# The first two groups of edges in another order, statistics by halves, and idle transposes, in a graph layer with experts

## What is computed

```python
xn = layernorm(x)                                   # no weights
m_in = concat([xn[src], edge_attr], axis=1)         # 2500 x 640
m = relu(m_in @ W1.T + b1) @ W2.T + b2
agg = segment_sum(m, dst, num_segments=10000)
gi = agg @ W_ih.T + b_ih                            # three gates of 512
gh = xn @ W_hh.T + b_hh
r = sigmoid(i_r + h_r); z = sigmoid(i_z + h_z); n = tanh(i_n + r * h_n)
h_new = (1 - z) * n + z * xn
x = x + xn + gamma * (h_new - run_mean) * rsqrt(run_var + 1e-5) + beta
x = x + top2_of_8_experts(layernorm(x)) + 0.5 * shared_expert
```

## Time and profile before

| | us |
|---|---|
| median of 3 runs | 1423.47 |
| lowest, highest | 1421.75, 1424.54 |
| the profiled execution's own time | 1422.28 |
| its span, first to last instruction | 1420.5 |
| PE busy | 1356.3 (95%) |
| DVE, ACT, POOL busy | 1030.6, 738.2, 827.6 |
| first matmul of `layer1(0)` | 23.34 |
| end of the last `sums` | 336.04 |
| first matmul of the nodes | 370.75 |

### The profile page before, as it was taken

The page is one execution under the profiler, slowest core; times in us unless marked ns, Lnnn a source line. Parts: engine busy times, 40 slices in busy tenths (PEclk is TensorE's granted clock), DMA queues, the critical chain, the costliest instruction groups (busy, mean ns, idle before and its releaser), DMA issues.

```text
span 1420.5 us, 22825 instructions
## 1 busy us (share of the span) xinstructions
PE 1356.3 (95%) x6398; PEld 1088.8 (77%) x6398; DVE 1030.6 (73%) x2194; ACT 738.2 (52%) x1665; POOL 827.6 (58%) x1119
## 2 busy tenths in 40 slices
PE   4889999999889999999999999999999999999996
PEld 3668888887668777877787778777777777777774
DVE  3586444233478888888888888888888888888885
ACT  3431323212466566656665666566666666666552
POOL 3210242103477777777777777777777777777771
PEclk9999999999989999999999999999999999999997
DMA  8222534246423333333333333333333333333330
GB/s 311 69 68 88 185 135 144 90 152 244 163 97 126 119 132 112 127 116 133 113 129 112 133 118 125 111 133 118 125 111 133 119 124 112 131 122 122 114 109 30
DMA packets 62863, 179.57 MB, mean 126 GB/s; under 512 B 9328, under 2 KB 9968, under 8 KB 62704
## 3 DMA queue, kind: packets, MB, share of 16 engines
q1 hardware_dynamic: 46912, 99.20, 20.4%
q0 software_dynamic: 15920, 79.97, 16.4%
HBM read 141.86 MB, written 37.29 MB: 126 GB/s over the span
## 4 chain that ended last, share of the span: by engine, by line
PE 89%; DVE 4%; issue 2%; DMA 1%; ACT 1%; POOL 1%; POOLq 0%; SPq 0%; DVEq 0%; ACTq 0%
PE bank L1547 45%; PE bank L1584 9%; PE bank L1214 8%; PE bank L1594 8%; PE bank L526 6%; PE bank L1166 5%; PE bank L1184 4%; PE bank L1197 3%; PE bank L1596 1%; POOL whh_lo_raw L766 1%; PE bank L1148 1%; DVE st_e L890 1%; DMA late_out<-gates_in,carry_at 1%; DMA whh_lo_raw<-in_whh_t 0%; DVE found L957 0%
## 5 line engine op out<-in xcount | busy, mean ns | idle before, releaser
L1547 PE MATMUL bank<-whh_hi,x_hi 128*128 128x512 f32 x948 | 382.5, 403 | 10.8 <-DVE x L1493 10.5
L1547 PE MATMUL bank<-whh_hi,x_lo 128*128 128x512 f32 x948 | 375.3, 396 | 0.0
L1547 PE MATMUL bank<-whh_lo,x_hi 128*128 128x512 f32 x948 | 375.2, 396 | 0.0
L1547 PEld LDWEIGHTS bank<-whh_hi,x_hi 128*128 128x128 f32 x948 | 178.5, 188 | 51.6 <-DVE x L1493 10.9
L1547 PEld LDWEIGHTS bank<-whh_hi,x_lo 128*128 128x128 f32 x948 | 178.4, 188 | 43.5
L1547 PEld LDWEIGHTS bank<-whh_lo,x_hi 128*128 128x128 f32 x948 | 178.7, 189 | 39.1
L1295 POOL TENSOR_TENSOR rstd<-var_eps,minus_half 128x1 f32<-128x1 f32 x158 | 90.6, 574 | 149.5 <-DVE var_eps L479 149.5
L1346 POOL TENSOR_TENSOR h_n<-h,n_gate 128x512 f32<-128x512 f32 x79 | 103.9, 1315 | 58.6 <-ACT n_gate L1402 58.6
L504 ACT ACTIVATE h<-xt,shift,rstd 128x512 f32<-128x512 f32 x79 | 64.5, 816 | 134.1 <-POOL one_rstd L1301 134.1
L1286 POOL DMA_INDIRECT gates<-gates_in,slot_at x79 | 85.3, 1079 | 60.0 <-issue 45.7
L1342 POOL TENSOR_TENSOR n_pre<-r_hn,gates 128x512 f32<-128x512 f32 x79 | 102.6, 1299 | 13.4 <-POOL r_hn L1338 13.2
(11 more groups left out here) (184 smaller groups left out, 3148.6 us busy)
## 6 DMA issues: line engine op xcount, KB each, us to landing
xt<-in_x SPq DMA_DIRECT2D x79, 256.0 KB, 2.9
x_lo_raw<-in_x_cols SPq DMA_DIRECT2D x79, 256.0 KB, 2.7
out<-y SPq DMA_DIRECT2D x79, 256.0 KB, 2.0
gates_in<-g_out SPq DMA_DIRECT2D x16, 768.0 KB, 4.0
wih_lo_raw<-in_wih_t SPq DMA_DIRECT2D x4, 768.0 KB, 15.7
whh_rows<-in_whh SPq DMA_DIRECT2D x4, 768.0 KB
whh_lo_raw<-in_whh_t SPq DMA_DIRECT2D x4, 768.0 KB, 7.5
gates_in<-late_out SPq DMA_DIRECT2D x6, 256.0 KB, 6.8
```

The lines of the kernel that those rows point to most:

```text
L1547: last = pe.matmul(to[0:R, :], a[:, s, k * R:(k + 1) * R], w[:, k, q * D:(q + 1) * D], start=n == 0, stop=n == 3 * DK - 1)
```

## The change

- **Halves.** For group 0, `stats`, `front` and `normalise` run for tiles 0 and 1, and then for tiles 2 and 3 (`HALVES`). On DVE both halves now stand ahead of the rest of W1's split and of the attributes' rest.
- **Banks.** The transposes of group 0 use four banks (2 to 5), and no longer wait for `transposed_lo`.
- **Idle transposes.** `keep_running(n)` is n transposes of the identity into bank 7, which nobody reads: 14 ahead of group 0's transposes, 8 behind them.
- **Moved up.** `compare(0)` and `stats(1)` stand between the `r_lo` of group 0; `normalise(1)` stands in halves behind ACT's blocks 2 and 3 of `layer1(0)`; PE turns tiles 0 and 1 of group 1 ahead of `layer2(0)`, tiles 2 and 3 behind it; the splits of these tiles stand between the messages of group 0.
- **W_ih.** Slices 0 and 1 are split ahead of and within `sums(0)`, slices 2 and 3 in the first two blocks of `layer1(1)`.
- **Last group.** The first product of the last group waits for each block of `a_lo` where it uses it, no longer for all four ahead of it.

The core of the diff:

```diff
+    HALVES = (slice(0, SUP // 2), slice(SUP // 2, SUP))
+    def bank_of_rows(g, j):
+        return bank[2 + (j if g == 0 else j % 2)]
...
-            front(0)
+            for of in HALVES:
+                front(0, of)
...
             for b in range(DK):
                 layer1(0, b)
-            normalise(1)
-            for j in range(SUP):
+                if b >= 2:
+                    normalise(1, HALVES[b - 2])
+            for j in range(2):
+                transposed_hi(1, j)
+            for j in range(2):
                 messages_hi(0, j)
             attributes_hi(1)
-            for j in range(SUP):
+            for j in range(2, SUP):
+                messages_hi(0, j)
+            for j in range(2, SUP):
                 transposed_hi(1, j)
+            wih_hi_of(0)
             for f in range(DK):
                 sums_hi(0, f)
+                if f == 0:
+                    wih_hi_of(1)
...
             dve.wait_ge(bias_done, 1)
-            sums_lo(0)
+            wih_lo_of(0)
+            sums_lo(0, slice(0, 1))
+            wih_lo_of(1)
+            sums_lo(0, slice(1, DK))
...
             def product(g, j):
-                if j == 0:
+                if j == 0 and g < NSUP - 1:
                     pe.wait_ge(a_lo_done, DK * (g + 1))
...
+                        if c == EC - SUP and q == 0:
+                            pe.wait_ge(a_lo_done, DK * g + k + 1)
...
+            def keep_running(n):
+                for _ in range(n):
+                    pe.transpose(bank[7][:, 0:P], ident[:, :], ident[:, :])
...
             pe.wait_ge(consts, 2)
+            keep_running(14)
             for j in range(SUP):
                 transposes(0, j)
+            keep_running(8)
             layer1(0)
+            for j in range(2):
+                transposes(1, j)
             layer2(0)
-            for j in range(SUP):
+            for j in range(2, SUP):
                 transposes(1, j)
             sums(0)
```

More of the change, by code:

```diff
@@ L685, in carry, with front @@
                                         ).then_inc(carried[s], 16)
-            def front(g):
-                pool.wait_ge(var_e, g + 1)
-                pool.tensor_tensor(rs_e[:, :], ve_e[:, :], minus_half[0:R, :], ALU.pow).then_inc(rs_ready, 1)
-                pool.wait_ge(rs_ready, g + 1)
-                pool.tensor_tensor(nmr_e[:, :], nm_e[:, :], rs_e[:, :], ALU.mult).then_inc(nmr_ready, 1)
+            def front(g, of=slice(0, SUP)):
+                n = fronts(g) if of.stop == SUP else g + 1
+                pool.wait_ge(var_e, n)
+                pool.tensor_tensor(rs_e[:, of], ve_e[:, of], minus_half[0:R, of], ALU.pow).then_inc(rs_ready, 1)
+                pool.wait_ge(rs_ready, n)
+                pool.tensor_tensor(nmr_e[:, of], nm_e[:, of], rs_e[:, of], ALU.mult).then_inc(nmr_ready, 1)
             def enter(c):
@@ L772, in hi_of, with normalise @@
                 return act.activation(hi, raw, ACT.Copy)
-            def normalise(g):
-                act.wait_ge(nmr_ready, g + 1)
-                for j in range(SUP):
+            def normalise(g, of=slice(0, SUP)):
+                act.wait_ge(nmr_ready, 1 if g == 0 and of.start == 0 else fronts(g))
+                for j in range(SUP)[of]:
                     act.activation(xs[:, j, :], xs[:, j, :], ACT.Identity, bias=nmr_e[:, j:j + 1],
@@ L819, in _ @@
             attributes_hi(0)
-            normalise(0)
+            for of in HALVES:
+                normalise(0, of)
             for j in range(SUP):
@@ L846, in _ @@
                     layer1(g, b)
-                    if g == 1:
-                        wih_hi_of(b)
+                    if g == 1 and b < 2:
+                        wih_hi_of(b + 2)
                     if 1 < g < NSUP - 1 and b == 2:
@@ L936, in layer2, with sums_lo @@
                 messages_lo(g, SUP - 1)
-            def sums_lo(g):
-                for f in range(DK):
+            def sums_lo(g, of=slice(0, DK)):
+                for f in range(DK)[of]:
                     dve.wait_ge(a_hi_done, DK * g + f + 1)
@@ L1036, in _ @@
                 layer1(0, b)
-            stats(1)
-            compare(0)
+                if b == 0:
+                    compare(0)
+                if b == 1:
+                    stats(1)
             dve.wait_ge(b2_in, 16)
-            layer2(0)
+            messages(0, 0)
+            for j in range(2):
+                transposed_lo(1, j)
+            messages(0, 1)
+            messages_lo(0, 0)
+            messages(0, 2)
+            messages_lo(0, 1)
             attributes_lo(1)
-            for j in range(SUP):
+            messages(0, 3)
+            messages_lo(0, 2)
+            messages_lo(0, 3)
+            for j in range(2, SUP):
                 transposed_lo(1, j)
```

45 lines of the change are left out of this document (28 added, 17 removed).

## The result

The changed kernel takes 1412.74 us (median of 4 runs, 1411.58 to 1413.07), the kernel before 1422.61 on the same chip (4 runs, 1421.54 to 1424.54): a ratio of 0.9930, with a 95% interval of 0.9917 to 0.9942, 9.9 us. The forecast was 9.1 us less and 1414.4, in a range of 1411.3 to 1418.5. Of the 1.7 us between 1414.4 and 1412.74, 0.9 is the base, 1423.47 as the median of three runs against 1422.61 of four, and 0.8 the gain.

What follows compares the result with a forecast made beforehand. PE's matmuls bound the node loop (busy 198.07 of 200 us), so only PE's waits in the edges could shrink. Terms 1 to 6 sum to 9.1 us, from 1423.47 to 1414.4, range 1411.3 to 1418.5.

Steps and rivals of the forecast that it cites:

- Term 1: Start of layer1(0): its first matmul moves from 23.34 to about 19.6, 3.7 us gained.
- Term 2: PE's clock in layer1(0): nine matmuls at a pitch of 0.23 instead of 0.43, 1.8 us gained.
- Term 3: From the end of layer1(0) to sums(0): 16.1 us instead of 18.1, new waits included, 2.0 us gained.
- Term 4: In sums(0), 7.40 us before: new waits for a_lo behind ig_bias and slices of wih_lo, 1.6 us lost.
- Term 5: In product(0,0): the wait of 2.5 for wih_lo goes, take_gates(0, 0) waits 0.8 instead of 0.3; 2.2 us gained.
- Term 6: Between edges and nodes: earlier DVE additions and whh_lo let POOL end at 359.2, not 360.2; 1.0 us gained (0 to 1.5).
- The rival of DVE as the bound: In the beginning: each new wait on DVE is twice as long, costing 5.1 us more, 1419.5; chance 0.14.

Runs made afterwards that it cites:

- another way between edges and nodes: Changed kernel with DVE instead of POOL subtracting the mean row from W_hh's last two slices, experts' weights split ahead of the first node's gates: 1410.44 us, ratio 0.9918.
- the other order around them: Changed kernel with group 1's transposes all behind layer2(0), its rows normalised behind block 3, a_lo(0) and a_lo(1) ahead of W_ih's slices: 1405.84 us, ratio 0.9889.

## Why the prediction was right, step by step

**Term 1** (3.7): 23.34 to 19.46, 3.9. The steps are there one by one: statistics of the first half done at 11.0, of the second at 12.9, third row at 14.84 (forecast 15.0). The second power ended at 14.53. I had it end with DVE's run of two instructions, at 14.8; the run ended at 14.59. Whether the power waited for the run or only for the `w_lo` that had started before it (ended 13.98, 0.55 ahead of the power's end) this row can't tell. A row of the run with another way between edges and nodes speaks for the one instruction:

```profile
339.80 2.12 POOL L1359 TENSOR_TENSOR rstd<-var_eps,minus_half 128x1 f32<-128x1 f32 x1
```

A power of 128x1, which takes 0.58 elsewhere, ends there at 341.92, 0.44 behind a `whh_lo` that had started before it and 0.17 ahead of the end of DVE's next instruction. `m_lo`, which DVE ran beside the second power, took its usual 0.69, so the power did not keep DVE out in turn. What I had worked out from the rule of the Trainium skill, SBUF — State Buffer, section "Who interferes with whom", a power that begins only behind both and `layer1(0)` at 20.7, didn't come; the rule speaks of the instruction under way and not of a run of them. In the later runs the wait for one instruction can be read off: 1.23 instead of 0.19 for the product, and the chain of 3.51, 1.6 and 3.4 us around `whh_lo`. Of the 3.9, only the halves were undone by a run (1.2); the share of the earlier place of the statistics and of the four banks is argued from the rows.

**Term 2** (1.8): 16.0 to 14.2 us for `layer1(0)` from its first matmul to its end, and 1.85 lost at the last `sums` without the idle transposes. The mechanism was right. What the prediction said of its price, "if not, nothing is lost", fits the changed kernel, where `layer1(0)` always began 0.1 behind the last `m_lo`, but only there: on the kernel before, the same transposes gave nothing (0.9997), and a longer row of them cost 2.8 us, and in the traces of both the clock fell in the waits ahead of `layer1(0)` or of `sums(0)`. By the Trainium skill, TensorE: Matmul & The Clock Gate, section "Part 4: PE-mode transpose", transposes don't count for the clock as matmuls do; here 14 transposes and nothing else stood ahead of the rise, and 46 likewise, so the measurement decides against it.

**Term 3** (2.0): 33.69 to 49.48 is 15.8 us, against 17.8 before. Its two new waits were forecast at 1.4 (with 0.3 for the second tile) and 1.3; in the timeline 0.98 stands ahead of the first tile's transposes, 0.3 within the eight (1.36 instead of 1.04), and 1.39 ahead of `sums`. Undoing it gave back 2.0 of these (2.15 with the later start).

**Term 4** (-1.6): `sums(0)` took 8.94 instead of 7.48 (between the first matmuls in the table), so -1.46. **Term 5** (2.2): from the first matmul of `layer1(1)` to the end of the last `sums` it took 271.40 before and 268.99 after, 2.4. The experiment that undid both moved the last `sums` by 0.97, their sum. The new wait for `g_out` in the third gate was 0.48, where the forecast reckoned 0.5 more; the longer one of 1.27 stood in the kernel before at 1.23. The two steps that term 5 names, 2.5 less and 0.5 more, make 2.0 and not 2.2, so the prediction has no source for 0.2 of it, nor does a row show where the measured 2.4 has its last 0.4.

The five make 8.6 at the last `sums`, where 8.1 was forecast: 0.2 from term 1, and 0.3 from terms 4 and 5.

**Term 6** (1.0): 34.71 to 33.69 from the last `sums` to the nodes, 1.0, and the run with the old wait gave 1.1 back, all of it, with the two rows on which the term was built, 4.89 and 5.02. POOL's pair, forecast to be held for 0.5 and then to take its own 7.0, took 7.28.

At the nodes' first matmul the steps make 9.7, where 9.1 was forecast. The rest up to 9.9 isn't a step of the sum: the node loop scatters by more than 1 us from execution to execution, with no change in it. The rival of DVE as the bound asked for new waits twice as long as forecast, and they came no longer: 1.0, 0.3, 1.4, 1.5 and 0.5, against 1.4, 0.3, 1.3, 1.6 and 0.5. But such waits set the distance to what was possible: the other order around them ends the last `sums` 5.2 us earlier, some 1.0 of it from a wait that the kernel before had too. They were in the forecast's terms, which is why it held, but the prediction took them as given.

## What to carry to other kernels

When work is moved up, list each instruction that now stands ahead of an operand of the bound engine, on the engine that makes it, and price each wait; here another order gave 5.2 us more where the whole change gave 9.9, by putting the operand first and the moved work behind it, and by leaving PE's own small work in a gap that another chain keeps open anyway. Warm a clock only right up to the work, and look at the waits that follow: here 14 idle transposes ahead and 8 right before the first product gave 1.85 us, while the same on a kernel with longer waits gave nothing, and a long row with waits of 1.7 and 1.5 behind it lost. Where two engines exclude each other, reckon with a queue of whole instructions, and check every short instruction in the chain, since one that needs 0.19 us can wait as long as one that needs 0.7.

## What the runs showed of the hardware

- Transposes alone raise PE's clock: the pitch went from 0.23 to 0.12 us behind 14 of them, and within a row of 46. With a break of 3.95 us behind the 14, the next eight ran at the low level (1.97).
- Equal work doesn't give an equal clock. With 2.41 us of work in 5, the clock stayed at 1.00 in the kernel before and was 0.57 in the next 3 us in the kernel with idle transposes alone. Eight idle transposes at the same place took 1.04 in one execution and 1.91 in another, and the matmuls behind them ran at the high level in both.
- POOL and DVE, both on operands in SBUF, took turns by instructions: a product of 128x2 that takes 0.19 took 1.23 behind a DVE instruction that had started 0.04 earlier, and ended 0.04 behind it. While DVE was on `bn_stats` the power took 0.73. A DVE subtraction that takes 1.75 took 4.89 behind a POOL one of 3.51.
